# Wavelet-token encoder block: subband weighting moved to ScalarE, the inverse column transform moved behind the inverse row transform

## The reference, cut to what matters

```python
for _ in range(3):
    cur, h, v, d = _dwt2(cur)           # Haar: sums and differences of columns, then of rows
    details.append((h, v, d))
aw = sigmoid(cur.reshape(B, -1) @ Wa + ba)
rec = cur * aw[:, :, None]
for (h, v, d), (Wd, bd) in zip(reversed(details), det_params):
    w = softmax(flat @ Wd + bd, axis=-1)
    rec = _idwt2(rec, h * w[:, 0], v * w[:, 1], d * w[:, 2])
h = concatenate([cls_tok, rec], axis=1)
h = h + attention(layernorm(h), R)      # softmax(mask + (x R) x^T) x, per image, 257 tokens of width 256
h = h + ffn(layernorm(h), ...)          # gate scores, top 1028 rows of each expert, two matmuls
```

## Time and profile before

| | |
|---|---|
| median of three executions | 887.17 us |
| profiled execution, time | 889.19 us |
| its span | 887.4 us |
| head (weights of the subbands) | to about 60 us |
| attention, 36 turns | about 60 to 337 us |
| search for the best rows | about 337 to 413 us |
| experts | about 413 to 887 us |
| busy share: TensorE, VectorE, ScalarE, GpSimd | 83, 66, 51, 52% |

### The profile page before, as it was taken

The page is one execution under the profiler, slowest core; times in us unless marked ns, Lnnn a source line. Parts: engine busy times, 40 slices in busy tenths (PEclk is TensorE's granted clock), DMA queues, the critical chain, the costliest instruction groups (busy, mean ns, idle before and its releaser), DMA issues.

```text
span 887.4 us, 15596 instructions
## 1 busy us (share of the span) xinstructions
PE 733.7 (83%) x4297; PEld 617.5 (70%) x4297; DVE 584.3 (66%) x1993; ACT 451.8 (51%) x996; POOL 461.1 (52%) x744
## 2 busy tenths in 40 slices
PE   5977999999999960012799897998989979989994
PEld 3644666677666740001699797998988979979994
DVE  2836888888888847888867475583655746644431
ACT  1003777777777762000554664565536655466552
POOL 0127676776777643202336547466465565645723
PEclk9987999999999995555899999998998999999997
DMA  9400122122221226101213423334232333333312
GB/s 345 180 3 1 48 72 71 48 71 71 71 71 48 72 72 144 64 0 37 67 25 49 126 44 90 79 51 131 43 97 68 51 96 72 58 116 49 49 20 30
DMA packets 45447, 64.30 MB, mean 72 GB/s; under 512 B 13840, under 2 KB 40528, under 8 KB 42704
## 3 DMA queue, kind: packets, MB, share of 16 engines
q1 hardware_dynamic: 32400, 46.54, 15.2%
q0 software_dynamic: 12800, 17.12, 11.8%
q10 hardware_dynamic: 192, 0.00, 0.0%
HBM read 38.12 MB, written 25.53 MB: 72 GB/s over the span
## 4 chain that ended last, share of the span: by engine, by line
PE 31%; issue 9%; DVE 8%; POOL 7%; DMA 4%; ACT 3%; POOLq 1%; DVEq 0%; ACTq 0%; SPq 0%
PE bank L873 15%; PE bank L887 12%; DMA raw<-in_fc1T 3%; POOL w2l L492 2%; POOL out L529 2%; POOL yg L507 2%; DVE ge L1195 2%; PE bank L862 1%; ACT bank L661 1%; PE bank L910 1%; PE bank L852 1%; PE bank L899 1%; DMA yg<-rows,idx 1%; ACT hh L664 1%; PE bank L837 1%
## 5 line engine op out<-in xcount | busy, mean ns | idle before, releaser
L1318 DVE TENSOR_TENSOR hl<-bank,hh 128x384 fp32r<-128x384 f32 (+1 forms) x192 | 97.6, 513 | 169.8 <-ACT hh L664 164.0
L529 POOL DMA_INDIRECT out<-ob,sidx x72 | 113.9, 1582 | 167.1 <-ACT ob L677 155.4
L661 ACT ACTIVATE bank<-bank,b1s 128x384 f32<-128x384 f32 (+1 forms) x192 | 99.5, 518 | 131.5 <-PE bank L873 126.4
L873 PE MATMUL bank<-yh,w1h 128*128 128x384 f32 (+1 forms) x384 | 137.6, 358 | 28.0 <-DVE hl L1318 26.8
L873 PE MATMUL bank<-yh,w1l 128*128 128x384 f32 (+1 forms) x384 | 127.6, 332 | 0.0
L873 PE MATMUL bank<-yl,w1h 128*128 128x384 f32 (+1 forms) x384 | 127.3, 331 | 0.0
L507 POOL DMA_INDIRECT yg<-rows,idx x72 | 72.2, 1002 | 72.2 <-issue 67.0
L887 PE MATMUL bank<-w2h,hh 128*128 128x256 f32 x384 | 108.4, 282 | 0.0
L887 PE MATMUL bank<-w2l,hh 128*128 128x256 f32 x384 | 108.3, 282 | 0.0
L887 PE MATMUL bank<-w2h,hl 128*128 128x256 f32 x384 | 108.2, 282 | 0.0
L873 PEld LDWEIGHTS bank<-yh,w1h 128*128 128x128 f32 x384 | 77.1, 201 | 33.0 <-DVE hl L1318 29.3
(11 more groups left out here) (219 smaller groups left out, 1738.3 us busy)
## 6 DMA issues: line engine op xcount, KB each, us to landing
BIG<-in_x SPq DMA_DIRECT2D x4, 2048.0 KB, 19.2
out<-Bs SPq DMA_DIRECT2D x32, 256.0 KB, 2.2
rows<-Yp SPq DMA_DIRECT2D x32, 256.0 KB, 2.4
raw<-in_fc1T SPq DMA_DIRECT2D x8, 1024.0 KB
raw<-in_fc2T SPq DMA_DIRECT2D x8, 1024.0 KB
yg<-rows,idx POOLq DMA_INDIRECT x72
out<-ob,sidx POOLq DMA_INDIRECT x72, 3.8
gwb<-in_gate_w SPq DMA_DIRECT2D x1, 1024.0 KB, 12.6
```

The lines of the kernel that those rows point to most:

```text
L529: g.indirect_dma_start(out=out_rows, out_offset=tok(ap=sidx[job.eh][0:m, t:t + 1], axis=0), in_=ob[t % 3][0:m, :], in_offset=None, compute ...
L661: A.activation(h[:, 0:cur.w], h[:, 0:cur.w], ACT.Gelu_apprx_tanh, bias=b1s[:, bass.ds(cur.e, 1), f]).then_inc(s["hact"], 1)
L873: last = T.matmul(Lb[ring(cur, f)][:, 0:cur.w], w1s[cur.eh][i][:, d, f * P:(f + 1) * P], yT[cur.p][k][:, d, 0:cur.w], start=(n == 0), stop ...
L1318: v.tensor_tensor(hT[cur.p][1][:, f, 0:cur.w], Lb[ring(cur, f)][:, 0:cur.w], hT[cur.p][0][:, f, 0:cur.w], ALU.subtract).then_inc(s["hlo"], 1)
```

## The change

The weighting goes to ScalarE: four copies from `Zb` to `Zw` with the weight as a pointer for the scale, widths 64, 64, 128 and 256 (both tiles together). ScalarE's copy of `Hb` to `hc` goes away. TensorE's matmul L771 now reads `Zw`, so the rows are inverted first, and VectorE inverts the columns of the result: a copy of 64 values out of PSUM and three pairs of additions and subtractions, each with one operand in `Hb` and one in SBUF, the last pair into `hc`. `bn_stats` reads `hc`, and so does ScalarE's `Ex`. `Q` is gone, `Zw` stays single; `Hb` is free once VectorE is through (`hcv`) instead of after `Ex`. GpSimd's block for the norms is split: the second norm's part (image m) first, `pow` on 128x4 values; then, behind the wait for `st0`, the first norm's part (image b): three instructions around a `pow` on 128x2, signalled as `nrm0`; both parts run in every turn. `columns` works two images ahead instead of one, behind both parts as before.

```diff
-        def steps(eng, emit):
+        def steps(eng, emit, ahead=1):
...
-                                       for d in range(1, -LAG - 1, -1)]
+                                       for d in (ahead, *range(0, -LAG - 1, -1))]
...
+                if m:
+                    po.wait_ge(s["st1"], m.n + 1)
+                apart(po)
+                g.tensor_scalar(A6[:, 2:4], st[:, 5:8:2], EPS, None, ALU.add)
+                g.tensor_scalar(nm[t.p][:, 2:4], st[:, 4:8:2], -1.0, None, ALU.mult)
+                g.tensor_scalar(A6[:, 4:6], st[:, 5:8:2], 1.0 + EPS, EPS * EPS, ALU.mult, ALU.add)\
+                    .then_inc(s["var"], 1)
+                po.wait_ge(s["var"], t.n + 1)
+                g.tensor_tensor(st[:, 10:14], A6[:, 2:6], mhalf[:, 0:4], ALU.pow).then_inc(s["pow"], 1)
+                po.wait_ge(s["pow"], t.n + 1)
+                apart(po)
+                g.tensor_tensor(N6[t.p][:, 2:4], st[:, 10:12], nm[t.p][:, 2:4], ALU.mult)
+                g.tensor_tensor(N6[t.p][:, 4:6], st[:, 12:14], nm[t.p][:, 2:4], ALU.mult)
+                g.tensor_scalar(O1[t.p][:, :], st[:, 10:12], 1.0, None, ALU.add).then_inc(s["nrm"], 1)
+
                 if b:
                     after(po, "hcE", b.n - 1)
                     po.wait_ge(s["st0"], b.n + 1)
...
+                g.tensor_scalar(A0[:, :], st[:, 1:4:2], EPS, None, ALU.add)
+                g.tensor_scalar(nm[t.p][:, 0:2], st[:, 0:4:2], -1.0, None, ALU.mult).then_inc(s["var0"], 1)
+                po.wait_ge(s["var0"], t.n + 1)
+                g.tensor_tensor(st[:, 8:10], A0[:, :], mhalf[:, 0:2], ALU.pow).then_inc(s["pow0"], 1)
+                po.wait_ge(s["pow0"], t.n + 1)
                 apart(po)
+                g.tensor_tensor(N6[t.p][:, 0:2], st[:, 8:10], nm[t.p][:, 0:2], ALU.mult).then_inc(s["nrm0"], 1)
                 if nxt:
                     columns(nxt)
...
             columns(Step(0, 0))
+            columns(Step(0, 1))
             po.wait_ge(s["st_set"], 2)
-            steps(po, emit)
+            steps(po, emit, 2)
...
-                if b:
-                    after(act, "h1", b.n - 3)
-                    act.wait_ge(s["st0_b"], b.n + 1)
-                    A.activation(hc[b.r][:, :, :], Hb[:, :].rearrange("p (h c) -> p h c", h=NH), ACT.Copy)
+                if a:
+                    after(act, "h0", a.n)
+                    act.wait_ge(s["z_done"], a.n + 1)
+                    apart(act)
+                    for g0, g1 in ((0, 1), (1, 2), (2, 4), (4, 8)):
+                        last = A.activation(Zw[:, :, g0 * 32:g1 * 32],
+                                            Zb[:, :].rearrange("p (h c) -> p h c", h=NH)[:, :, g0 * 32:g1 * 32], ACT.Copy,
+                                            scale=W8[:, bass.ds(a.n, 1), g0])
+                    last.then_inc(s["zw"], 1)
...
-                    act.wait_ge(s["nrm"], t.n + 1)
+                    act.wait_ge(s["nrm0"], t.n + 1)
                     for h in range(NH):
-                        last = A.activation(Ex[b.r][:, h, 0:D], Hb[:, h * D:(h + 1) * D], ACT.Identity,
+                        last = A.activation(Ex[b.r][:, h, 0:D], hc[b.r][:, h, :], ACT.Identity,
...
-                    after(pe, "hcE", b.n)
-                    pe.wait_ge(s["q"], b.n + 1)
-                    T.matmul(Hb[:, :], cst("inv"), Q[b.p].rearrange("p h c -> p (h c)"), start=True, stop=True)\
+                    after(pe, "hcv", b.n)
+                    pe.wait_ge(s["zw"], b.n + 1)
+                    T.matmul(Hb[:, :], cst("inv"), Zw.rearrange("p h c -> p (h c)"), start=True, stop=True)\
...
+                    after(dve, "h1", b.n - 3)
                     dve.wait_ge(s["h0"], b.n + 1)
+                    H = Hb[:, :].rearrange("p (h c) -> p h c", h=NH)
+                    dst = hc[b.r]
+                    v.tensor_copy(I3[:, :, :], H[:, :, 0:32]).then_inc(s["inv"], 1)
+                    dve.wait_ge(s["inv"], b.n * 3 + 1)
+                    v.tensor_tensor(I2[:, :, 0::2], I3[:, :, :], H[:, :, 32:64], ALU.add)
+                    v.tensor_tensor(I2[:, :, 1::2], I3[:, :, :], H[:, :, 32:64], ALU.subtract).then_inc(s["inv"], 1)
+                    dve.wait_ge(s["inv"], b.n * 3 + 2)
+                    v.tensor_tensor(I1[:, :, 0::2], I2[:, :, :], H[:, :, 64:128], ALU.add)
+                    v.tensor_tensor(I1[:, :, 1::2], I2[:, :, :], H[:, :, 64:128], ALU.subtract).then_inc(s["inv"], 1)
+                    dve.wait_ge(s["inv"], b.n * 3 + 3)
+                    v.tensor_tensor(dst[:, :, 0::2], I1[:, :, :], H[:, :, 128:256], ALU.add)
+                    v.tensor_tensor(dst[:, :, 1::2], I1[:, :, :], H[:, :, 128:256], ALU.subtract).then_inc(s["hcv"], 1)
+                    dve.wait_ge(s["hcv"], b.n + 1)
                     for h in range(NH):
-                        last = v.bn_stats(bn0[:, h, :], Hb[:, h * D:(h + 1) * D])
+                        last = v.bn_stats(bn0[:, h, :], dst[:, h, :])
...
-                if a:
-
-                    dve.wait_ge(s["z_done"], a.n + 1)
...
```

More of the change, by code:

```diff
@@ L158, in build_program @@
         Zw = cut(NH * D).rearrange("p (h c) -> p h c", h=NH)
+        I3 = cut(NH * 32).rearrange("p (h c) -> p h c", h=NH)
         I2 = cut(NH * 64).rearrange("p (h c) -> p h c", h=NH)
         I1 = cut(NH * 128).rearrange("p (h c) -> p h c", h=NH)
-        Q = [cut(NH * D).rearrange("p (h c) -> p h c", h=NH) for _ in range(2)]
         Ex = [cut(NH * DG).rearrange("p (h c) -> p h c", h=NH) for _ in range(4)]
@@ L182, in build_program @@
         ST = [sb(f"ST{i}", [P, 16]) for i in range(2)]
+        A0 = sb("A0", [P, 2])
         A6 = sb("A6", [P, 6])
@@ L225, in build_program @@
             cls_d cls_p cls_a cls_t et0 et_cls g_cls cls_st cls_g zero
-            xc xc_l z_done zw inv q h0 st0_b st0 var pow nrm st_set hcE et et_ev er er_ev eg_ev sm nmax pexp pt pt_ev av u h1 rv
+            xc xc_l z_done zw inv hcv h0 st0_b st0 var pow nrm var0 pow0 nrm0 st_set hcE et et_ev er er_ev eg_ev sm nmax pexp pt pt_ev av u h1 rv
             st1_b st1 tug teg base yp tab base_st0 base_st1 yp_st0 yp_st1
@@ L584, in _, with emit @@
             A.activation(z2[:, 0:1], zz[:, 0:1], ACT.Exp, scale=-1.0).then_inc(s["z_e"], 1)
-            def emit(t, _nxt, _a, b, c, d, m):
+            act.wait_ge(s["w8"], 1)
+            def emit(t, _nxt, a, b, c, d, m):
                 if d:
@@ L782, in emit @@
                 if a:
-                    after(pe, "zw", a.n * 2)
+                    after(pe, "zw", a.n)
                     pe.wait_ge(s["xc"], a.n + 1)
@@ L1085, in emit @@
                     v.reciprocal(ST[1 - t.p][:, 14:16], rsm[d.p][:, :]).then_inc(s["rv"], 1)
-                if a:
-                    dve.wait_ge(s["z_done"], a.n + 1)
-                    for g0, g1 in ((0, 2), (2, 8)):
-                        w = W8[:, bass.ds(a.n, 1), g0:g1].to_broadcast([P, NH, g1 - g0]).unsqueeze(3)\
-                            .to_broadcast([P, NH, g1 - g0, 32])
-                        v.tensor_tensor(Zw.rearrange("p h (g c) -> p h g c", g=8)[:, :, g0:g1, :],
-                                        Zb[:, :].rearrange("p (h g c) -> p h g c", h=NH, g=8)[:, :, g0:g1, :], w,
-                                        ALU.mult).then_inc(s["zw"], 1)
-                    dve.wait_ge(s["zw"], a.n * 2 + 1)
-                    lo, hi = Zw[:, :, 0:32], Zw[:, :, 32:64]
-                    v.tensor_tensor(I2[:, :, 0::2], lo, hi, ALU.add)
-                    v.tensor_tensor(I2[:, :, 1::2], lo, hi, ALU.subtract).then_inc(s["inv"], 1)
-                    dve.wait_ge(s["zw"], a.n * 2 + 2)
-                    dve.wait_ge(s["inv"], a.n * 2 + 1)
-                    hi = Zw[:, :, 64:128]
-                    v.tensor_tensor(I1[:, :, 0::2], I2[:, :, :], hi, ALU.add)
-                    v.tensor_tensor(I1[:, :, 1::2], I2[:, :, :], hi, ALU.subtract).then_inc(s["inv"], 1)
-                if a:
-                    dve.wait_ge(s["inv"], a.n * 2 + 2)
-                    after(dve, "h0", a.n - 1)
-                    hi = Zw[:, :, 128:256]
-                    v.tensor_tensor(Q[a.p][:, :, 0::2], I1[:, :, :], hi, ALU.add)
-                    v.tensor_tensor(Q[a.p][:, :, 1::2], I1[:, :, :], hi, ALU.subtract).then_inc(s["q"], 1)
                 if d:
```

13 lines of the change are left out of this document (removed).

## The result

Four executions of the changed kernel took 902.33 to 904.08 us, median 903.76; the kernel before, beside it, 885.32 to 889.79, median 887.93. The ratio is 1.0184, 95% interval 1.016 to 1.0208: **slower by 16 us**, and inside the range of 889 to 910. The predicted 899.5 was 4.3 us too low. The profiled execution has a span of 901.7 us (before 887.4).

The account below looks back on a forecast made before the run. A ring over two turns (VectorE, GpSimd, ScalarE, TensorE, VectorE) was taken to bind: 2.18 - 1.37 + 0.06 = +0.87, +0.43 a turn, +12.6 over 29 turns; with -1.5 and +1.3, +12.4 on 887.17 gives 899.5 us, range 889 to 910.

Parts of the forecast that it names:

- The ring: Wait chain VectorE, GpSimd, ScalarE, TensorE, VectorE, closing over two turns: 16.02 us read, 15.62 without a stall; chance 0.72.
- TensorE is the bound: Rival: TensorE's queue sets the turn, so removed waits save 0.35 x 29 = 10 us, some 877; chance 0.09.
- +2.18 for the combination: VectorE's inverse columns between row matmul and statistics: 1.75 for the steps, 0.32 copy, 0.11 last wait, in us.
- -1.37 for the split: GpSimd's norm block: image m's part hidden, so `Ex` waits 1.72 us behind `st0` instead of 3.09.
- +0.06 for `Ex` from SBUF: ScalarE's two `Ex` activations: 1.08 us from SBUF against 1.02 from PSUM.
- The ring term, +12.6: Turns 4 to 32: +0.87 us for two turns, +0.43 a turn, over 29 turns.
- VectorE against GpSimd: Rival: L1124, two SBUF inputs, stalls 0.4 us by GpSimd every turn; +4 to +6 us, 904 to 906; chance 0.10.
- -1.5 for the start: First turns: L771 no longer waits for `Ex`, so its transposes go first; -1.5 us (0 to -2.5).
- +1.3 for the end: Last turn: nothing hides GpSimd's second part, so VectorE's table work waits 1.3 us more for L481.
- Weighting nothing: ScalarE ahead of L612: 1.1 us of weighting fits in 1.4 to 1.5; uncovered, at most 0.2 a turn.
- columns nothing: `columns` two ahead removes L786's wait of at most 0.3 us, in TensorE's queue, so worth nothing.
- a fall of the clock in the stage: Sign of being wrong: TensorE's clock dropping in the attention stage, where it was forecast unchanged at full.

Follow-up runs that it names:

- yp_first: The changed kernel with `Yp` ahead of `Ex` on ScalarE, `Bs` still behind `Ex`; 891.69 us, ratio 1.0063 to the kernel before.
- late: The kernel before with `Yp` and `Bs` one turn later, ahead of `Ex`, `Ex` from `hc`, and `Hb` free once copied; 882.48 us, ratio 0.9948.
- repeat: The changed kernel with three of the combination's `tensor_tensor` instructions issued twice, the second time into an unread tile; 909.96 us, ratio 1.0257 to the kernel before.
- one_block: The changed kernel with GpSimd's norm block whole again, behind `st0`; 919.73 us, ratio 1.0381 to the kernel before.
- cols2: The kernel before with only `columns` moved to two images ahead; 888.61 us, ratio 1.0021.
- split_alone: The kernel before with only GpSimd's norm block split, `Ex` in its old place; 895.18 us, ratio 1.0092.
- dve_weights: The changed kernel with the weighting back on VectorE as two multiplications, off ScalarE; 900.45 us, ratio 1.0139 to the kernel before.
- no_columns: The changed kernel with GpSimd's column transform left out for images 2 to 31; 899.12 us, ratio 1.0148 to the kernel before.

## Why the prediction was right, point by point

- **The ring sets the turn.** Shown by yp_first and late, which shorten it and gain, by repeat and one_block, which lengthen it and lose 0.4 of that per turn, and by cols2, where TensorE's spare time shows and the turn stays. "TensorE is the bound" would have kept the wait at L812 as it was; it is 0.84 us where I forecast 0.7. TensorE's share is nine tenths at full clock, as forecast.
- **+2.18 for the combination.** From L1093's start to L1105's it took 215.95 - 214.00 = 1.95 us: the copy with its wait 0.26 (I took 0.32), the six steps 1.65 (1.75), the last wait 0.04 (0.11). A PSUM operand costs nothing: L1098 0.29 and L1102 0.41 beside 294 ns and 0.42 from SBUF. The Trainium skill (VectorE: DVE Perf Modes, the TRN2 errata) would add 65 ns to each by my estimate; the trace doesn't bear this out.
- **-1.37 for the split.** one_block gives 1.35. It holds only because the combination hides the first part: GpSimd sat idle for 0.45 us between the parts. split_alone has no such cover, and there the split costs 0.31 a turn. The change without the split costs 1.03 a turn (one_block) and the split without the rest 0.31; together they cost 0.45, so neither price taken alone would have told the sum.
- **+0.06 for `Ex` from SBUF.** That leg grew by 0.08.
- **The ring term, +12.6.** Turns 4 to 32 took +12.6. The exact agreement is in part luck and hides small errors: per turn it was +0.45 against +0.43, since the first leg grew by 0.71 and not 0.81, and the stall pair by 0.14, which I had counted at nothing. That is the mechanism of the rival "VectorE against GpSimd", at a third of its price: L1130 took 1.24 to 1.57 us in the turns around 210 to 228, beside 0.88 when GpSimd is quiet. The steady turns (8.41 against 7.92) lost a little more than +0.43, the first ones less.
- **-1.5 for the start**: -1.8. **+1.3 for the end**: +1.3; L1169 waited 4.64 us where it had waited 3.29.
- **Weighting nothing, columns nothing.** dve_weights and cols2 say so, for the steady turn.
- **The step that failed: the sum prices only turns 4 to 32, and turns 33 and 34 stand at nothing.** They cost +3.0 us. Turn 33 took 10.02 us instead of 7.48: of these 2.5, 1.5 are matmuls at a lower clock (rows in the section on the hardware), and I read the 1.0 left over as the lengthened ring, which reaches one turn further than I had counted: in dve_weights, where the clock stayed full in turn 33, that turn took 334.94 - 326.63 = 8.31, 0.8 more than before. Turn 34 took 0.44 more, and all of it lies behind the start of L827, 344.69 - 341.67 = 3.02 us to L1122 where it was 330.92 - 328.34 = 2.58 (L809 before): the clock fell there in both kernels, but in the changed one in time to slow L827 too. With these 3.0, and less the 0.3 that the start gained beyond the forecast, the sum gives +15.1, which is what the trace has.

The prediction named a fall of the clock in the stage as a sign of being wrong. It fell in the last two turns, and some 2 of the 3.4 us by which the forecast increase (12.4) fell short of the measured one (15.8) are that. In the steady turns it stayed at 1.00. The table work starts 15.1 us later, the profiled executions lie 14.3 apart (903.50 and 889.19), the medians 15.8.

## What to carry to other kernels

An engine at 98% of a stretch need not be what bounds it. Follow one item round every engine until you are back at the start, and divide by the number of turns that this takes: a step on that ring costs its length over that number, and a step off it costs nothing, however long. A split of a block of work gains only if something hides the first half, so it must be priced with the step that gives the cover. When a ring is shortened, the next one doesn't show in the shares of busy time: look for the buffer that the moved step frees. And the cheapest gain was in the order of one queue: two steps with slack (`Yp` and `Bs`) stood between two steps without.

## What the hardware showed that I had not expected

**TensorE's clock in the drained pipeline.** Turn 33 of after, L820 in turns 32 and 33, and then the windows of 4 us (columns as in the earlier trace rows):

```profile
323.40 1.97 PE L820 MATMUL bank<-ET,Rw 128*128 128x256 f32 x8
...
331.58 0.88 PE L812 MATMUL bank<-C,ARENA 128*128 128x128 f32 x3 [2.13 <-ACT ARENA L608]
332.25 3.14 PE L820 MATMUL bank<-ET,Rw 128*128 128x256 f32 x8
```
```profile
328.00:332.00 4.00, 1.29 (x8) 0.87 (x7) 2.29 (x10) 3.92 (x11) 1.73 (x6) 0.92 0.11 37
332.00:336.00 4.00, 4.00 (x15) 3.32 (x14) 0.00 (x0) 1.06 (x3) 2.27 (x9) 0.65 0.27 96
```

TensorE had been busy for 1.29 of 4 us, with a wait of 2.13 us for the exponentials, and the granted clock then fell from 1.00 (2.4 GHz) towards 0.5 (1.2 GHz). The eight matmuls of L820 took 3.14 us instead of 1.97, and L812 0.88 instead of 0.52: 1.5 us, more than half of what turn 33 lost. In the kernel before, the corresponding window was busier and the clock stayed:

```profile
316.00:320.00 4.00, 2.28 (x17) 1.71 (x15) 3.42 (x12) 3.94 (x11) 0.67 (x4) 1.00 0.13 43
```

In turn 34 both kernels wait 2.16 us before L812 (L794), which still runs in 0.52 us, and the clock falls only behind it. Before, then after:

```profile
327.09 0.52 PE L794 MATMUL bank<-C,ARENA 128*128 128x128 f32 x3 [2.16 <-ACT ARENA L595]
328.34 0.79 PE L809 MATMUL bank<-ARENA 128*128 128x264 f32 x2 [0.73 <-ACT ARENA L605]
```
```profile
340.41 0.52 PE L812 MATMUL bank<-C,ARENA 128*128 128x128 f32 x3 [2.16 <-ACT ARENA L608]
341.67 1.22 PE L827 MATMUL bank<-ARENA 128*128 128x264 f32 x2 [0.73 <-ACT ARENA L618]
```

The Trainium skill (TensorE: Matmul & The Clock Gate, Part 1) describes a gate that halves the clock of an array that has been idle; the trace agrees, with 1.00 and 0.50 as the two levels, and the falls of turns 33 and 34 come behind waits of 2.1 to 2.2 us. In turn 33 the clock also fell in one_block, repeat and no_columns, where the eight matmuls took 3.62, 3.65 and 3.65 us. It did not in dve_weights, with the same wait of 2.13 us. So in the drain of a pipeline a longer wait can cost twice, but need not: the length of the wait alone doesn't tell. What decides is open, as no experiment kept TensorE busy there.

**VectorE stalls behind GpSimd by fractions that move with the phase.** The same pair of `scalar_tensor_tensor` with two SBUF inputs took 0.88 us with GpSimd quiet, 0.92 in the mean in one_block and repeat, 1.15 before, 1.29 after and up to 1.57 singly (1.69 in dve_weights). The pair L1122, with one of its inputs in PSUM, took 0.89 us in every row shown. Shifts of GpSimd's work moved 0.1 to 0.4 us on or off the ring, which is why the longer first leg of one_block and repeat reached the turn by less than half. The Trainium skill (GPSIMD Engine Reference, Specifications) names such VectorE instructions as contending for the shared interface; the trace agrees.
